# Fewer writes of zeros between gathers, and 880 tiles instead of 888 in four scatter passes of a graph network kernel

## The reference, cut to what matters

```
h6   = relu(segment_sum((x @ W6)[src] * norm, dst) + b6)     # pass 1: weighted by edge
h7   = relu(segment_sum((h6 @ W7)[src] * norm, dst) + b7)    # pass 2: the same edges
...                                                          # a layer with channel gates, no big pass
msgs = silu([x[row], x[col]] @ W1.T + b1) @ W2.T + b2
agg  = segment_sum(msgs, row) / count                        # pass 3, then a GRU cell
mf   = segment_sum((x @ W_f.T)[row] * ew, col)               # pass 4: 128 features
mb   = segment_sum((x @ W_b.T)[col] * ew, row)               # pass 5: 128 features
```

## Time and profile before

| | |
|---|---|
| median of 3 runs | 7920.8 us (7919.51 to 7923.13) |
| the profiled execution | 7923.1 us, of which the span is 7921.4 us |
| TensorE busy | 5616.0 us (71%), mean granted clock 0.744 of full |
| GpSimd busy | 5609.5 us (71%) |
| VectorE busy | 4543.2 us (57%) |
| ScalarE busy | 1859.7 us (23%) |
| pass 1, gathers issued | 271.7 to 1692.3 us |
| pass 2 | 1796.5 to 3141.5 us |
| pass 3 | 3686.4 to 4984.2 us |
| passes 4 and 5 | 5452.7 to 6653.0, 6654.9 to 7855.7 us |

### The profile page before, as it was taken

How to read it: one execution, slowest core, us unless ns; L and a number is a source line. 1 busy time by engine, 2 the same in 40 slices (tenths; PEclk the granted TensorE clock), 3 DMA queues, 4 the chain that set the end, 5 groups by cost and what they waited for, 6 DMA issues and landing times. The chain is left out here.

```text
span 7921.4 us, 135935 instructions
## 1 busy us (share of the span) xinstructions
PE 5616.0 (71%) x23276; PEld 3616.4 (46%) x23277; DVE 4543.2 (57%) x12188; ACT 1859.7 (23%) x3217; POOL 5609.5 (71%) x8005
## 2 busy tenths in 40 slices
PE   5566666678999998898777777797555555555554
PEld 4433333445555554676444545454333333333332
DVE  8876666546666666796666666465333333443334
ACT  4100000016666664104333333342000000000000
POOL 0388888848888888003888888104888888888885
PEclk8577666689999998859999999897555555555555
DMA  2243333333222222133323223311221113111112
GB/s 87 46 110 103 105 104 106 110 86 121 87 87 87 86 87 76 42 117 127 90 89 90 90 89 89 77 34 44 60 61 52 49 49 47 48 48 49 49 49 66
DMA packets 310618, 612.40 MB, mean 77 GB/s; under 512 B 90042, under 2 KB 164102, under 8 KB 310344
## 3 DMA queue, kind: packets, MB, share of 16 engines
q0 software_dynamic: 185408, 469.86, 22.4%
q1 hardware_dynamic: 125064, 141.13, 5.9%
HBM read 566.94 MB, written 50.13 MB: 78 GB/s over the span
## 5 line engine op out<-in xcount | busy, mean ns | idle before, releaser
L871 PE MATMUL bank<-ring,oh 128*128 128x128 f32 x3552 | 1400.8, 499 | 1015.4 <-DMA ring<-fwd_table,stage_i 396.4
L871 PEld LDWEIGHTS bank<-ring,oh 128*128 128x128 f32 x3552 | 888.1, 311 | 1528.2 <-DVE acc L1864 937.2
L1864 DVE TENSOR_TENSOR acc<-bank,acc 128x128 f32 x1776 | 518.0, 292 | 1317.2 <-PE bank L871 1312.2
L608 POOL MEMSET tile_oh<- 128x256 f32 x3512 | 1169.3, 333 | 1.8
L620 POOL DMA_INDIRECT ring<-h_table,stage_i x888 | 893.2, 1006 | 265.2 <-POOL tile_oh L608 145.6
L1828 DVE TENSOR_TENSOR acc<-bank,acc 128x256 f32 x1776 | 753.7, 424 | 534.6 <-PE bank L944 447.1
L620 POOL DMA_INDIRECT ring<-fwd_table,stage_i x888 | 845.7, 952 | 271.7 <-issue 187.8
L620 POOL DMA_INDIRECT ring<-bwd_table,stage_i x888 | 845.1, 952 | 212.9 <-issue 118.0
L1289 ACT ACTIVATE ring<-big 128x889 f16<-128x889 f16 x840 | 874.0, 1041 | 401.7 <-PE bank L955 397.5
L955 PE MATMUL bank<-ring,big 128*128 128x445 f16 (+1 forms) x3360 | 774.2, 352 | 0.0
L1839 DVE TENSOR_SCALAR oh<-iota,d_loc,d_norm 128x128 f32<-128x128 f32 x1776 | 705.1, 401 | 75.8 <-DVE big L1936 20.3
(11 more groups left out here) (438 smaller groups left out, 7992.1 us busy)
## 6 DMA issues: line engine op xcount, KB each, us to landing
big<-places_in_block SPq DMA_DIRECT2D x111, 256.0 KB
acc<-places_in_block SPq DMA_DIRECT2D x74, 384.0 KB
ring<-h_table,stage_i POOLq DMA_INDIRECT x888, 2.8
ring<-fwd_table,stage_i POOLq DMA_INDIRECT x888, 2.5
ring<-bwd_table,stage_i POOLq DMA_INDIRECT x888, 2.5
big<-x_and_degree,stage_i POOLq DMA_INDIRECT x536, 2.8
h_table<-hq SPq DMA_DIRECT2D x50, 128.0 KB, 1.7
x_table<-ring SPq DMA_DIRECT2D x25, 256.0 KB, 2.1
```

The source lines that it names most:

```text
L608: pool.memset(spacer, 0.0).then_inc(S["spaced"], 1)
L871: pe.matmul(bank[u % 4][:, 0:width], oh[:, u % 4, :], gbuf[:, u, 0:width], start=True, stop=True).then_inc(S["mm"], 1)
L1864: dve.tensor_tensor(to, bank[u % 4][:, 0:width], to, ALU.add).then_inc(S["accd"], 1)
```

## The change

A tuple `EVERY = (2, 2, 2, 2, 2)` says after which gathers of each pass the write of zeros stands: after every second, in all five. So it changes passes 1, 2 and 3; in passes 4 and 5 it was so before. `WRITES` numbers the writes across the passes.

Passes 2 to 5 run `TILES` = 880 tiles (`OCT` = 110 octets) instead of 888: 36 full turns of 24 and one of 16 (`REST`). Pass 1 keeps 888. All semaphore counts that were made from `T` in these passes are made from `before_pass`. The last turn of pass 2, in which VectorE adds the bias in 25 pieces, has 16 tiles instead of 24. The helpers of pass 3 take a last turn with some groups of its own.

```
-def runs(g, lag, first, last):
-    return g >= lag if first else g < lag if last else True
+def runs(g, lag, first, last, groups):
+    return g >= lag if first else g - lag < groups if last else True
...
+    OCT = -(-T_MAX // RING)
+    TILES = OCT * RING
+    FULL_TURNS, REST = TILES // SPAN, TILES % SPAN
+    REST_GROUPS = REST // GROUP
+    before_pass = lambda k: T + TILES * (k - 1) if k else 0
...
+        EVERY = (2, 2, 2, 2, 2)
+        WRITES = [0] + [(T - LONG) // EVERY[0] + sum(TILES // EVERY[p] for p in range(1, k)) for k in range(1, 5)]
...
             def gathers(k, table, width, free, base):
-                with pool.Fori(0, TURNS) as i:
-                    for u in range(SPAN):
+                def some(i, tiles):
+                    for u in range(tiles):
...
-                        if k == 1:
-                            space(i * SPAN + u + T - LONG)
-                        elif u % 2:
-                            space(i * (SPAN // 2) + u // 2 + 3 * T - LONG + T // 2 * (k - 3))
+                        if (u + 1) % EVERY[k] == 0:
+                            space(i * (SPAN // EVERY[k]) + u // EVERY[k] + WRITES[k])
+                with pool.Fori(0, FULL_TURNS) as i:
+                    some(i, SPAN)
+                some(FULL_TURNS, REST)
...
-                    if not first:
-                        space((i - 1) * LONG + u)
+                    if not first and (u + 1) % EVERY[0] == 0:
+                        space((i - 1) * (LONG // EVERY[0]) + u // EVERY[0])
...
-                    space(i * SPAN + u + T - LONG + T)
+                    if (u + 1) % EVERY[2] == 0:
+                        space(i * (SPAN // EVERY[2]) + u // EVERY[2] + WRITES[2])
...
             def scatter_pass(k, kk, width):
-                with pe.Fori(0, OCTETS) as i:
+                with pe.Fori(0, OCT) as i:
...
             second_pass(J // SPAN, False, True)
-            with pe.Fori(J // SPAN + 1, TURNS) as i:
-                second_pass(i, False, False)
+            second_pass(FULL_TURNS, False, False, REST)
...
-            in_turns(pe, TURNS, l2_products, 2)
+            in_groups(pe, FULL_TURNS, l2_products)
...
                 def add_bias(i, u):
-                    for n in range(u * PAIRS // SPAN, (u + 1) * PAIRS // SPAN):
+                    for n in range(u * PAIRS // REST, (u + 1) * PAIRS // REST):
...
-                scatter_turn(TURNS - 1, 1, d_loc, d_norm, blk_d, 0, D, add_bias)
+                scatter_turn(FULL_TURNS, 1, d_loc, d_norm, blk_d, 0, D, add_bias, SPAN, REST)
```

More of the change, by code:

```diff
@@ L700, in _, with third_gathers @@
             pool.wait_ge(S["x2t_out"], 16 * PAIRS)
-            with pool.Fori(0, TURNS) as i:
-                for u in range(SPAN):
+            def third_gathers(i, tiles):
+                for u in range(tiles):
                     v = u // RING
@@ L933, in _, with second_pass @@
                 pe.matmul(bank[b][:, 0:HALF], ident_b[:, :], zeros.bitcast(BF16)[:, 0:HALF], start=True, stop=False, skip_group_check=True)
-            def second_pass(i, own, earlier):
-                for u in range(SPAN):
-                    n = i * SPAN + T + u
+            def second_pass(i, own, earlier, tiles=SPAN):
+                for u in range(tiles):
+                    n = i * SPAN + before_pass(1) + u
                     v, r = u // RING, u % RING
@@ L1067, in l2_products @@
             def l2_products(i, first, last):
-                for g in range(2 if last else GROUPS):
+                for g in range(REST_GROUPS + 2 if last else GROUPS):
                     m = i * GROUPS + g
-                    if runs(g, 1, first, last):
+                    if runs(g, 1, first, last, REST_GROUPS):
                         h = g - 1
@@ L1090, in l2_products @@
                         mm.then_inc(S["l2_t"], 1)
-                    if runs(g, 2, first, last):
+                    if runs(g, 2, first, last, REST_GROUPS):
                         for u in range(GROUP):
@@ L1306, in _ @@
                 raise_turn(i, False)
-            for octet in range(J // RING + 2, OCTETS):
+            for octet in range(J // RING + 2, OCT):
                 stage_again(octet, octet % 3, d_idx, 1)
@@ L1395, in _, with l2_functions @@
             staggered(act, PAIRS, 10, d4_functions)
-            def l2_functions(i, first, last, ending=False):
-                for g in range(1 if last else GROUPS):
-                    if not last:
+            def l2_functions(i, first, last):
+                for g in range(REST_GROUPS + 1 if last else GROUPS):
+                    if not last or g < REST_GROUPS:
                         act.wait_ge(S["l2_t"], i * GROUPS + g + 1)
@@ L2189, in l2_sums @@
             def l2_sums(i, first, last):
-                for g in range(3 if last else GROUPS):
-                    if not last:
+                for g in range(REST_GROUPS + 3 if last else GROUPS):
+                    if not last or g < REST_GROUPS:
                         dve.wait_ge(S["l2_c"], i * SPAN + 4 * g + 4)
```

81 lines of the change are left out of this document (44 added, 37 removed).

## The result

| | before | changed |
|---|---|---|
| median | 7921.97 us (7919.51 to 7925.65, 4 runs) | 7561.77 us (7561.54 to 7562.62, 4 runs) |
| the profiled execution | 7923.1 us, span 7921.4 us | 7561.54 us, span 7559.8 us |

The ratio is 0.9545, with a 95% interval of 0.953 to 0.956. The change gained 360 us. The forecast was 280 us, with a range that ended at 7612 us, so the direction and the place were right and the size was too small by 80 us.

What follows compares the result with a forecast made beforehand. GpSimd was taken to set the pace: 246 us from fewer writes, plus 39.7 for the eight tiles, minus 6 for late consumers, gave 280 us saved, so 7641 us. The 80% range was 7612 to 7725 us.

Steps and rivals of the forecast that it cites:

- GpSimd sets the pace, and the others can follow: Passes 1 to 3: GpSimd never waits for TensorE in pass 2; steps fall to 1.49, 1.415 and 1.36 us a tile.
- The 6 us taken off for late consumers: Passes 1 to 3: estimated loss for moments when VectorE's own chain is late, 0 to 80 us possible.
- the 11.1 us in 7 waits of 1.6: Pass 1: the part of GpSimd's 93 us idle time that was put down to TensorE.
- The write's worth, 0.193 us a pair: Passes 1 to 3: each pair of gathers with one write less saves 0.193 us; 1296 pairs give 250 us.
- the long second gather (8250 us): Passes 1 to 3: a pair's second gather takes 1.430 us instead of 0.952, making the kernel slower; 5%.
- one lost pass (7720): Pass 2 stays where it is because TensorE and VectorE can't follow, losing 79 us; another engine taking over one pass had 15%.
- Rival "slower": Passes 1 to 3: gathers with no write between them are long gathers, so the kernel takes 8250 us; 5%.
- the second rival: Passes 1 to 3: the consumers' chain binds once GpSimd is quicker, so only the tiles' 39.7 us remain, 7881 us; 6%.
- The stalls: GpSimd's waits of 1.6 and 2.1 us, nine or ten a pass, possibly rarer; with a stretched write up to 25 us more.
- Stretched gathers: Pass 2: VectorE's sort steps lengthen gathers, 47 us in all, rising to 51, so 4 us are lost.
- The eight tiles: Ends of passes 2 to 5: eight tiles fewer each save 39.7 us together, 21.6 of them in passes 4 and 5.
- Pass 2's last turn: End of pass 2: VectorE's bias adds, one-hots and sums set the pace; eight tiles fewer save 6.4 us.

Runs made afterwards that it cites:

- g1: Changed kernel with the write after every gather in all passes, 343 instead of 256 columns wide; pass 3 took 1.536 us a tile.
- g2: Changed kernel with its write after every second gather made 654 bfloat16 columns long; 0.973 of the kernel before, which took 8577 us there.
- g4: Changed kernel with the write after every gather in all passes, 300 columns wide; 8423 us, where the kernel before took 8577.
- h1: Changed kernel with 654-bfloat16-column writes after every second gather and two more GpSimd counts after each gather; 8273 us against 8375 for the kernel before.
- f1: The kernel before, unchanged, run for its own trace on a slower chip; 8362 us.
- c1: The changed kernel itself, unaltered, on a slower chip; 8535 us, 2.0% slower than the kernel before there.
- h2: The changed kernel itself, unaltered, on a slower chip; 8545 us against 8375 for the kernel before.
- f3: Changed kernel with the 256-column write after every gather in all five passes; 8298 us.
- e6: Changed kernel with two more counts by GpSimd after each gather; 43 us beyond the changed kernel on a slower chip.

## Why the prediction was wrong, by its own steps

- *GpSimd sets the pace, and the others can follow.* Right on the chip of the result. In the stretches of passes 2 and 3 read there, GpSimd waits for no other engine of the changed kernel, and TensorE follows at 1.397 us in pass 2. The 6 us taken off for late consumers weren't lost. One reading was wrong: the 11.1 us in 7 waits of 1.6 that the prediction lays on TensorE in pass 1 are stalls.
- *The write's worth, 0.193 us a pair.* Right as a term: the gap is 0.30, the second gather 0.95, and there are 2184 writes. No run on that chip measures writes and tiles apart. None of the rivals came true; the long second gather (8250 us) and one lost pass (7720) didn't occur. Rival "slower" had 5%: on the chip of the result it was far off, but the change does cost 2% on the two other chips where it was run itself, where the other engines don't keep up: the second rival's kind of wait, but with a loss that no rival had.
- *The stalls.* This is the term that was mis-sized. The prediction named the waits of 1.6 and 2.1 us, nine or ten a pass, as something that might become rarer, and gave them, with a stretched write, 25 us of the lower bound and nothing of the sum. They were 28 in passes 1 to 3, 49.7 us, and 1 was left (1.8 us): 48 us, put at nothing in the sum. The trace of before held what was needed: passes 4 and 5, where a write follows every second gather, had none. g1, g2, g4 and h1, on other chips, show that they go with the write after every gather.
- *Stretched gathers.* Wrong in sign. The prediction added 4 us in pass 2, since gathers would fill more of the time. The mean fell from 1006 to 999 ns there (14.0 us less, 8 of them for the eight tiles), and in pass 1, where no term stood, the sum fell by 20.4 us. With pass 3, where they fell by 4 us beyond its eight tiles, that is about 34 us against the forecast. In h1, with the long write, pass 1's mean is 973 ns, and in g1 with twice as many writes 1021; how VectorE's steps and the gathers come to lie isn't shown further.
- *The eight tiles.* Passes 4 and 5 gave 13.9 us instead of 21.6, since their step rose slightly, from 1.353 to 1.354 and 1.361; there the gathers' mean went from 952 to 954 and 960 ns.
- *Pass 2's last turn.* The prediction called it VectorE's, worth 6.4 us. But GpSimd had no wait in it except behind its writes, and issued its 24 gathers in 37.0 us. From its first gather to its last sum that turn took 45.1 us before and 32.1 in the changed kernel, 13.0 us less.
- The account of the missing 80 us: stalls 48, gathers 20 in pass 1, 10 in pass 2 and 4 in pass 3, consumers 6, passes 4 and 5 -8. That is 80. What pass 2's last turn gave beyond its 6.4 us is offset by small differences elsewhere, among them the writes of passes 2 and 3, whose mean was 0.329 us and not 0.333.

The rule of the Trainium skill that the prediction weighed (SBUF — State Buffer, "Who interferes with whom", which infers that a tensor_tensor doesn't hold up descriptor writing) isn't borne out by the changed kernel either: the 1.33 us gather above stands beside such a step. In pass 2 of the kernel before, the 366 gathers beside a sort step last 1.068 us at the mean, the other 522 last 0.962.

The range was too narrow below: it gave the stalls and a stretched write 25 us together, though the sum of the stalls over three passes, 49.7 us, stood in the trace.

## What to carry to other kernels

Count the small periodic holes of the engine that sets the pace (waits of over 1 us), also those that the profile lays on an engine that had long been done, and look whether the passes that already have the new pattern have them. If not, their whole sum belongs in the forecast.

A change that speeds up one engine should be timed on more than one chip: here it gave 4.5% on one and cost 2% on two others. Where the others don't keep up, a slower producer is worth a try: 5% more time a tile on GpSimd went with a pass 3 that was 5% quicker (1.615 to 1.536 us, across two chips on which the kernel before takes 8362 and 8372 us).

Before "issue" is read as "nothing was awaited", count the semaphore records. With 49,187 updates instead of 114,119 it hid a wait of TensorE for VectorE, which only the times of the instructions and packets brought out.

## What the runs showed of the hardware that was not expected

- The same kernel took 7922 us on one chip and 8362 to 8577 on five others, with gathers of 0.952 us, writes of 0.33 and gaps of 0.305 at the median on all. In pass 4 TensorE has 112 holes of over 3 us on f1's chip and none on the result's; each ends with a one-hot of VectorE's, and VectorE has 583 register instructions of some 0.69 us there. In pass 3 GpSimd waits for ScalarE's index octets.
- VectorE has not one long register instruction when GpSimd needs 1.52 us a tile or more (g1, g2, h1). It has 1264 and 1202 in the changed kernel (c1, h2), where GpSimd needs 1.35, and 340 at 1.45 (f3); on the chip of 8577 us there were 379 at 1.50. With two counts more after each gather (e6) there were 417 at the changed kernel's pace.
- Where GpSimd sets the pace, it stalls for 1.5 to 2.1 us some 8 to 11 times a pass when a write follows every gather, and 0 or 1 times when it follows every second, at 1.35 to 1.52 us a tile, and also with two counts more after each gather.
- A write of zeros costs 0.33 us for 256 float32 columns, 0.37 for 300, 0.40 for 343, 0.125 for 8, and 0.67 for 654 bfloat16 columns: by the column, not by the byte.
- The trace of the kernel before from a slower chip holds 49,187 of its semaphore updates, that from the result's chip 114,119, with all 135,935 instructions in both.
